# The epsilon of a head norm moved into a spare column of its squares, in an attention and expert-FFN kernel

## What is computed

```python
EPS = 1e-06
def _qknorm(t, scale):
    norm = jax.lax.rsqrt(jnp.mean(t * t, axis=-1, keepdims=True) + EPS)
    return t * norm * scale
q = _qknorm(q, q_scale)
k = _qknorm(k, k_scale)
scores = jnp.einsum('bhtd,bhsd->bhts', q, k) * scale      # causal softmax, times v, times Wo
x = x + attention(mix1(x)); x = x + ffn(mix2(x))
```

## Time and profile before

| what | value |
|---|---|
| median of 3 runs | 420.47 us (418.64 to 420.99) |
| the profiled execution, its own time | 419.07 us |
| its span in the profile | 417.3 us |
| around the span | 1.8 us |
| TensorE busy | 367.4 us (88%) |
| VectorE busy | 331.4 us (79%) |
| ScalarE busy | 275.9 us (66%) |
| GpSimd busy | 218.5 us (52%) |
| granted TensorE clock, mean | 0.996 |

### The profile page before, as it was taken

How to read it: one execution, slowest core, us unless ns; L and a number is a source line. 1 busy time by engine, 2 the same in 40 slices (tenths; PEclk the granted TensorE clock), 3 DMA queues, 4 the chain that set the end, 5 groups by cost and what they waited for, 6 DMA issues and landing times.

```text
span 417.3 us, 6425 instructions
## 1 busy us (share of the span) xinstructions
PE 367.4 (88%) x1952; PEld 294.3 (71%) x1952; DVE 331.4 (79%) x779; ACT 275.9 (66%) x673; POOL 218.5 (52%) x229
## 2 busy tenths in 40 slices
PE   0098778899999789898998987999899999999995
PEld 0097566688878667687776876687587878888884
DVE  8999788999988997789999889486557777665543
ACT  5547778798889498696976887785375434453321
POOL 7160613179524858225585121464259756888831
PEclk9999989999999999999999999999999999999999
DMA  7735300113100304001031000111065343274121
GB/s 214 297 87 183 104 0 0 52 52 102 53 0 2 102 0 137 15 3 50 2 101 40 1 2 0 38 41 38 2 160 172 138 126 81 97 218 173 53 75 50
DMA packets 14209, 31.92 MB, mean 76 GB/s; under 512 B 1872, under 2 KB 4432, under 8 KB 14176
## 3 DMA queue, kind: packets, MB, share of 16 engines
q1 hardware_dynamic: 13888, 31.38, 23.6%
q10 hardware_dynamic: 288, 0.14, 0.1%
HBM read 30.43 MB, written 1.08 MB: 76 GB/s over the span
## 4 chain that ended last, share of the span: by engine, by line
PE 53%; DVE 25%; ACT 15%; issue 5%; POOLq 0%; POOL 0%; DVEq 0%; ACTq 0%
PE ov L1223 6%; PE sc L1201 5%; PE acc L1126 4%; PE acc L1127 4%; PE acc L1128 4%; PE tr L1152 4%; ACT PR L623 4%; DVE B L868 3%; DVE F L868 3%; DVE PR L1062 3%; PE proj L1140 3%; PE tr L1128 2%; PE tr L1126 2%; PE tr L1127 2%; PE sc L1126 2%
## 5 line engine op out<-in xcount | busy, mean ns | idle before, releaser
L596 POOL TENSOR_TENSOR WL<-stage,WH 128x256 fp32r<-128x256 f32 x142 | 125.9, 916 | 75.1 <-ACT WH L662 75.1
L610 POOL TENSOR_TENSOR PR<-PR,RI 128x512 f32<-128x512 f32 x48 | 53.6, 1133 | 83.8 <-DVE RI L1072 83.8
L1140 PE MATMUL proj<-WH,RH 128*128 128x512 f32 x96 | 42.5, 443 | 33.0 <-DVE RL L921 19.9
L1126 PE MATMUL acc<-OH,WH 128*128 128x256 f32 (+1 forms) x172 | 54.5, 317 | 2.9 <-DVE OL L1084 2.2
L623 ACT ACTIVATE PR<-PR,MX 128x128 f32<-128x128 f32 (+1 forms) x128 | 56.9, 458 | 0.0
L1127 PE MATMUL acc<-OL,WH 128*128 128x256 f32 (+1 forms) x172 | 53.1, 309 | 0.0
L1128 PE MATMUL acc<-OH,WL 128*128 128x256 f32 (+1 forms) x172 | 53.0, 308 | 0.0
L1201 PEld LDWEIGHTS sc<-kT,QT 128*128 128x128 f32 x256 | 41.6, 193 | 16.1 <-issue 12.9
L1201 PE MATMUL sc<-kT,QT 128*128 128x128 f32 (+1 forms) x256 | 47.8, 330 | 0.0
L1223 PE MATMUL ov<-PTS,V 128*128 128x512 f32 x96 | 46.6, 594 | 1.1 <-DVE OL L1084 1.1
L1140 PEld LDWEIGHTS proj<-WH,RH 128*128 128x128 f32 x96 | 18.4, 192 | 39.5 <-issue 37.2
(11 more groups left out here) (160 smaller groups left out, 878.4 us busy)
## 6 DMA issues: line engine op xcount, KB each, us to landing
stage<-in_ffn SPq DMA_DIRECT2D x22, 384.0 KB, 3.3
stage<-in_wq SPq DMA_DIRECT2D x8, 512.0 KB, 3.3
stage<-in_wo SPq DMA_DIRECT2D x8, 512.0 KB, 3.4
SBC<-group_scalars SPq DMA_DIRECT2D x8, 256.0 KB, 3.6
PR<-in_tables SPq DMA_DIRECT2D x4, 352.0 KB, 7.2
fT<-in_fT SPq DMA_DIRECT2D x4, 256.0 KB, 3.8
xT<-in_xT SPq DMA_DIRECT2D x4, 256.0 KB, 4.1
stage<-in_wk SPq DMA_DIRECT2D x2, 512.0 KB, 4.7
```

What stands on the lines that cost most here:

```text
L596: i = pool.tensor_tensor(lo[:, c:c + 256], src[:, c:c + 256], hi[:, c:c + 256].bitcast(F32), ALU.subtract)
L610: pool.tensor_tensor(pr, pr, RI[:, m % 4, hs[0]:hs[0] + nh].rearrange("p (h o) -> p h o", o=1).broadcast_to([P, nh, 512 // nh]), ALU.mult) ...
L1126: mm(o, lh, rh, start=first, stop=False, skip_group_check=True)
L1140: mm(proj[:], rh[ch], wh[ch], start=ch == 0, stop=False, skip_group_check=True)
```

## The change

The tile `SQ` gets 129 columns a head instead of 128. GpSimd writes D * EPS into the 129th column of both buffers once, at the start; ScalarE writes the squares into the first 128. VectorE sums all 129, so SS is D times the variance with the eps in it. The instruction that made VAR is gone, and with it the tile. Ln reads SS and is given the scale 1/D; the first Newton instruction reads SS and has 0.5/D for 0.5. ScalarE now waits for the second sum of a pair. VectorE waits once, ahead of the first sum, for the new column. Apart from that, three K3 steps stand one tick later in the plan: K3 of tile 3 of pair 0 in tick 6 for 5, K3 of tiles 0 and 1 of pair 1 in ticks 17 and 18 for 16 and 17.

```diff
-    for half, places in (((0, 1), [2, 4, 4, 5, 5]), ((1, 0), [15, 15, 15, 16, 17]), ((1, 1), [17, 18, 18, 19, 19])):
+    for half, places in (((0, 1), [2, 4, 4, 5, 6]), ((1, 0), [15, 15, 15, 17, 18]), ((1, 1), [17, 18, 18, 19, 19])):
...
+NORM_END = [e for q, e in TOK.items() if q[-1] % 2]
...
-        SQ = sb("SQ", [P, 2, REP * D])
+        SQ = sb("SQ", [P, 2, REP, D + 1])
...
-        SS, VAR, LN, Y0, NA_, NB_, RQ = (sb(n, [P, NST, 2, REP]) for n in ("SS", "VAR", "LN", "Y0", "NA_", "NB_", "RQ"))
+        SS, LN, Y0, NA_, NB_, RQ = (sb(n, [P, NST, 2, REP]) for n in ("SS", "LN", "Y0", "NA_", "NB_", "RQ"))
...
             i.then_inc(s["bmask_ready"], 1)
+            pool.memset(SQ[:, :, :, D:D + 1], D * EPS).then_inc(s["eps_ready"], 1)
...
-                    nc.scalar.activation(SQ[:, e % 2, :], proj[:], ACT.Square).then_inc(s["square_ready"], 1)
+                    nc.scalar.activation(SQ[:, e % 2, :, 0:D], proj[:].rearrange("p (h n) -> p h n", h=REP), ACT.Square).then_inc(s["square_ready"], 1)
...
-                    act.wait_ge(s["var_ready"], n + 1)
-                    nc.scalar.activation(LN[:, n % NST, :, :], VAR[:, n % NST, :, :], ACT.Ln).then_inc(s["act_link"], 1)
+                    act.wait_ge(s["sumsq_done"], NORM_END[n] + 1)
+                    nc.scalar.activation(LN[:, n % NST, :, :], SS[:, n % NST, :, :], ACT.Ln, scale=1.0 / D).then_inc(s["act_link"], 1)
...
-                v.tensor_reduce(SS[:, n % NST, half_, :], SQ[:, e % 2, :].rearrange("p (h n) -> p h n", h=REP), X,
-                                ALU.add).then_inc(s["sumsq_done"], 1)
-                if half_:
-                    dve.wait_ge(s["sumsq_done"], e + 1)
-                    v.tensor_scalar(VAR[:, n % NST, :, :], SS[:, n % NST, :, :], 1.0 / D, EPS, ALU.mult, ALU.add).then_inc(s["var_ready"], 1)
+                if e == 0:
+                    dve.wait_ge(s["eps_ready"], 1)
+                v.tensor_reduce(SS[:, n % NST, half_, :], SQ[:, e % 2, :, :], X, ALU.add).then_inc(s["sumsq_done"], 1)
...
-                y, a, b_, r, var = (x[:, n % NST, :, :] for x in (Y0, NA_, NB_, RQ, VAR))
-                linked(v.scalar_tensor_tensor(out=a, in0=y, scalar=0.5, in1=var, op0=ALU.mult, op1=ALU.mult))
+                y, a, b_, r, total = (x[:, n % NST, :, :] for x in (Y0, NA_, NB_, RQ, SS))
+                linked(v.scalar_tensor_tensor(out=a, in0=y, scalar=0.5 / D, in1=total, op0=ALU.mult, op1=ALU.mult))
```

More of the change, by code:

```diff
@@ L426, in program @@
         wkv_act wkv_dve tanh1_done r1_ready r2_ready tanh2_done base_gated rh2_done
-        proj_full tr_full tok_ready square_ready sumsq_done var_ready rs_act rq_ready kn_ready q_turned k_turned v_ready table_full tables_cleared table_hi table_lo
+        proj_full tr_full tok_ready square_ready sumsq_done eps_ready rs_act rq_ready kn_ready q_turned k_turned v_ready table_full tables_cleared table_hi table_lo
         scores_full max_ready exp_done rinv_ready p_ready pt_act pt_dve ov_full o_hi o_lo wo_done x1_ready
```

## The result

The changed kernel takes 415.75 us (median of 6 runs, 415.53 to 416.55) against 419.69 us (418.64 to 420.99, 6 runs) for the kernel before: ratio 0.9914 [0.989, 0.9938], 3.6 us less by the ratio and 3.9 by the medians. The forecast was 416.5. The kernel before scatters in two groups: of 11 runs of a later comparison seven lay at 418.46 to 419.43 and four at 420.12 to 420.68. The profiled execution of before (419.07) belongs to the lower group; against that one alone the changed kernel's profiled execution (415.53) gains 3.5 us, the span 3.6 (417.3 to 413.7).

The account below looks back on a forecast made before the run. No single engine was taken as the bound: the chain of waits lay 53% on TensorE, 25% on VectorE, 15% on ScalarE. Gains of 2.3 + 1.2 + 0.7 - 0.2 = 4.0 us gave 416.5 from the median 420.47, range 413.5 to 419.9.

Parts of the forecast that it names:

- signs that were to show me wrong: New TensorE wait in tick 6 for VectorE's copy of D, scans of 1.7 us for 1.2, or SQ at 700 ns.
- Removal of VAR: Norm: 20 VectorE instructions removed, seven of them on the chain of waits, worth 2.3 us with semaphore steps.
- seven prices: VARs on the chain: 0.17, 0.18, 0.18, 0.26, 0.49, 0.17 and 0.68 us, plus some 0.03 us semaphore step each.
- the 13 at nothing: The other VARs, costed at nothing because ScalarE's exponentials or a full TensorE cover them; worth at most 4.3 us more.
- After the VARs of 144.44 and 215.11 ScalarE's Ln is the next on the path … gained whole: Ln touches nothing of GpSimd's, so the wait is not passed on and 0.49 and 0.68 us are gained.
- A rider to it: At 59.27 the first Newton instruction reads two SBUF tiles, so 0.08 us of GpSimd wait would pass to it.
- The longer sum and the gapped write: VectorE's 40 sums over 516 elements charged 0.2 us in all; ScalarE's squares with gaps charged nothing, 2 us allowed.
- The rival of a costly write: ScalarE's gapped write costs 0.2 us on each of 20 squares, 4 us, cancelling the gain: 420.5 us; chance 0.06.
- K3 at tick 5: K3 of tile 3 moved to tick 6: query copy 1.7 us earlier, 0.5 paid back in tick 6, net 1.2 us.
- K3 at tick 16: K3 of pair 1 moved: bank alternation shifts, D 1.1 us earlier, 0.4 paid back in tick 18, net 0.7 us.
- More comes through: Rival: half of the 4.3 us of the 13 VARs costed at nothing is gained too, 414.4 us; chance 0.16.
- Slower: GpSimd's bursts fall on other work: Rival: shifted bursts hit VectorE scans, some 0.5 us each; 13 newly hit give 423.0 us; chance 0.09.

Follow-up runs that it names:

- norm_only: Changed kernel with the three K3 steps back in their old ticks: 417.49 us, ratio to before 0.9965.
- dead_var: Changed kernel with the VAR instruction issued again at its old place on VectorE, read by nobody: 417.04 us, ratio to before 0.9944.
- swap16: norm_tick5 with K3 and the D of item 12 exchanged in tick 16 on TensorE and ScalarE: 416.30 us, ratio to before 0.9925.
- dead_reduce: dead_var with a tensor_reduce in place of the unread tensor_scalar on VectorE: 416.74 us, ratio to before 0.9934.
- moves_only: Kernel before with the three K3 steps one tick later and VAR kept: 417.39 us, ratio to before 0.9966.
- act_step: Changed kernel with a second, useless Ln of SS on ScalarE ahead of each Ln: 416.28 us, ratio to before 0.9925.
- norm_tick5: Changed kernel with the K3 steps of pair 1 back in ticks 16 and 17: 416.21 us, ratio to before 0.9939.
- late_keys: Changed kernel with K3 of tile 3 of pair 1 in tick 20 for 19: 416.54 us, ratio to before 0.9932.

## Why the prediction was right

**Sign and size.** The forecast lay 0.75 us above the result. That it lay above is partly luck: two errors ran against each other. The sum was 4.0 us and 3.5 were gained on the profiled execution (415.1 forecast, 415.5 measured), so the sum was 0.5 too large. The forecast then added the 1.4 us by which the first three runs' median lay above that execution, and the changed kernel has no upper group to match: its 12 runs lie between 415.53 and 416.55. VectorE's busy time fell by 5.1 us (5.4 in the second profile) for 5.7. One of the signs that were to show me wrong did come, a new wait of TensorE in tick 6 for VectorE's copy of D, but of 0.23 us only.

**Removal of VAR: right at its places, mis-sized as a whole.** The term was 2.3 us, less 0.2 for the longer sum; norm_only gained 1.4. Its leads grow by 0.9 up to 63 (30.10 to 59.27, priced at 0.17 + 0.18 + 0.18 + 0.26 and 0.12 of steps, 0.91), by 0.5 at 147 (0.52), by 0.2 at 202 (0.20), by 0.7 at 217 (0.71). So all seven prices hold and the 13 at nothing gave nothing that shows. What was missing is a term for giving back: 0.2 us between 98 and 119, 0.1 between 154 and 172, 0.4 between 217 and 302, and 0.3 behind 302, 1.0 us in all. I had charged such a term for the moves and none for the norm. The last 0.3 is not taken back by a later bound at all: it is the slower pace of TensorE's products in the feed-forward part (last section), a stretch in which no instruction was changed and for which the prediction had no term.

**"After the VARs of 144.44 and 215.11 ScalarE's Ln is the next on the path … gained whole".** The size at 215 was right, the mechanism was not. The chain of before goes on from VAR to ScalarE, and I took that path for the only one. In dead_var it is as short as in the changed kernel and nothing is gained: VectorE's own queue, with the copy behind VAR, is just as late. At 144 us the step holds for the query copy. A rider to it, that the Newton instruction behind the VAR at 59.27 would inherit 0.08 us (by the rows 0.26 - 0.17 = 0.09), did not come about: that instruction took 0.17 us in both. It was misread as the next one. Ln and Exp stand between them, so in before it starts at 60.03, when GpSimd's multiplication has been over since 59.48.

**The longer sum and the gapped write.** The sum takes 3 ns more, where 5 had been charged; the write costs nothing. The rival of a costly write has fallen. (Its bound had been worked out as 2 us, of which only 1.5 went into the upper end of the range; nothing hangs on it here.)

**K3 at tick 5.** Priced 1.7 gained at the query copy, 0.5 given back, 1.2 net. Measured: 1.7 gained (0.9 to 2.6), 0.6 back by 98, 1.3 net by the times and 1.1 by the leads at 302. Only 0.2 of the 0.6 is back by 80, in tick 6, where I had put all of it; which instruction takes the rest I have not traced.

**K3 at tick 16.** Priced 1.1 gained, 0.4 back in tick 18, 0.7 net. Measured: 0.9 gained, 0.4 to 0.5 back by 172 beyond what the norm gives back there (the 1.89 us wait shown above), 0.4 net. The D did wait for the copy that frees at 150.08 in before's time, as said; that the alternation of banks as such brings it has been refuted by swap16.

**Rivals.** "More comes through" needed gains at the other 13: none. "Slower: GpSimd's bursts fall on other work" needed scans newly hit. The scans of the changed kernel, against the earlier trace rows:

```profile
L870 DVE TENSOR_TENSOR_SCAN B<-DEC,E x16: 1197/1205/1997, 7.4 to 236.3; 128x514 f32<-128x514 f32 x16
```

In both kernels the same 13 of 32 scans take over 1.5 us, and all take 45.9 and 45.8 us in total. They moved together with GpSimd's bursts.

## What to carry to other kernels

Price a removed small instruction place by place on the chain of waits, then subtract a share for what later bounds take back: here three tenths to a half of what each part gained was gone by the end of the attention. If nobody waits for an instruction, it still costs its place on a full engine, which a copy of it without a reader measures directly. Keep the same tiles in both kernels of such a comparison, since taking one away moves the others in SBUF, and here the totals then differed by 0.4 us more. When steps share two buffers in turn, count the turns between a slow reader and the next user, and before moving one look at what the slow reader is queued behind.

## What the hardware showed that I had not expected

**The Newton instructions wait for GpSimd as well.** The first two of a pair, NA_ and NB_, read two SBUF tiles, 8 numbers a partition. In the changed kernel five of these 40 start while a subtraction of GpSimd is running, and three of the five are long; two are from one pair in the timeline of VectorE and GpSimd:

```profile
41.94 2.12 POOL L598 TENSOR_TENSOR WL<-stage,WH 128x256 fp32r<-128x256 f32 x3
...
43.10 0.29 DVE L938 SCALAR_TENSOR_TENSOR NA_<-Y,SS 128x8 f32<-128x8 f32 x1 [0.52 <-ACT Y L625]
43.43 0.65 DVE L939 TENSOR_TENSOR NB_<-NA_,Y 128x8 f32<-128x8 f32 x1
```

The third is a NA_ of 0.37 us at 70.97. In before one NB_ took 0.58 and no NA_ over 0.17; the NA_ group has gone from 3.3 to 3.7 us busy. It would be easy to read that as VAR's wait passed down to the next instruction. It isn't: dead_var and dead_reduce, which have an instruction in VAR's place, show the same long ones (NA_ 0.31 and 0.35, 0.29 and 0.36 us; NB_ 0.65 and 0.65), and moves_only, with VAR itself, has a NA_ of 0.33 us at 71.83. What changed is where these instructions fall against GpSimd's subtractions.

**The unchanged feed-forward part became slower.** From the first to the end of the last L1108 it takes 100.24 us in before and 100.22 in moves_only. In the nine profiles of kernels in which the tile VAR is gone and SQ is 32 bytes a partition larger it takes 100.55 to 100.80. In the three that keep the tile VAR (dead_var, dead_reduce, act_step) it is 100.33 to 100.48. TensorE sets the pace there, with next to no gaps (0 to 0.6 us in all), and its matmuls follow each other at other distances: from the third pass of an output product to the first of the next 234.1 ns in before, 237.5 in the changed kernel and 232.8 in dead_var. That one distance is 0.07 us in all. But if every kind of neighbouring pair that occurs 15 times or more is taken, without the pairs that have a wait between them, the distances add up to 0.39 to 0.42 us more than in before in each of the nine profiles, and to between -0.01 and 0.04 us in moves_only and the three that keep the tile. So the slowdown goes with the tiles and not with the instruction: act_step has no VAR instruction on VectorE either, and has before's pace.

The instructions are the same; what differs is where the later tiles lie in SBUF (96 bytes a partition lower, or 32 higher). That the addresses are the cause was not tried. It is worth 0.4 us, as much as the tick 16 move, and accounts for the 0.3 us that norm_only loses behind 302. It also means that the total times set the losses of dead_var, dead_reduce and act_step against the changed kernel some 0.4 us too low. Whether the changed kernel with an unused tile in VAR's place would be 0.4 us faster is the open question; no run has it.

**A low clock that cost nothing.** In before, TensorE stood still 2.35 us up to 58.29, and from 58 to 62 us its granted clock was 0.57 as the mean of the stretch, near the lower of the levels 1.2 and 2.4 GHz. In the changed kernel it stood still 2.16 us, and the clock stayed up. The length of the stop does not tell the two apart: norm_tick5, dead_var and late_keys stood still 2.14 us and have the low clock, norm_only stood still 2.14 us and has not. First the stretch's row of before, then two of the changed kernel (us, PE, PEld, DVE, ACT, POOL, clock, DMA):

```profile
58.00:62.00 4.00, 3.71 (x10) 2.94 (x10) 3.34 (x14) 2.57 (x8) 1.49 (x2) 0.57 0.00 0
```

```profile
54.00:58.00 4.00, 1.84 (x10) 1.37 (x10) 3.35 (x17) 3.20 (x11) 1.13 (x2) 1.00 0.00 0
58.00:62.00 4.00, 3.06 (x14) 2.27 (x12) 3.38 (x10) 3.27 (x9) 0.91 (x1) 1.00 0.00 0
```

TensorE is busy 3.06 us there where it was 3.71 at the low clock, but then waits 1.20 us for the query copy at 62.26. norm_tick5, which has the low clock in its profile (0.58 in the same stretch), leads by 0.8 us at 63 and 2.6 at 70, the changed kernel by 0.9 and 2.6. So no part of the gain at these places comes from it.
